# A norm aggregated early, Fourier steps placed elsewhere and stores of two images in a four-layer convolution kernel

## Chip, cores and metric

One core of one Trainium2 chip. The metric is the device time of one execution in microseconds (us), lower is better; the time before is the median of three runs.

## The reference, cut to what matters

The input is 8 images of 32 channels and 64 x 64 points. A first block makes nine softmax weights per point and filters x with them. Then four layers follow, each in this form:

```python
for j in range(4):
    z = conv3x3(x, Kj)
    z = relu(batchnorm(z, gamma[j], beta[j]))          # the first norm of the layer
    x = x + 0.1 * conv3x3T(z, Kj)
    x = batchnorm(x, gamma[j], beta[j])                # the second norm
    x = real(ifft2(fft2(x) * t))                       # t from Lj, one table for each channel
```

Both norms take mean and variance over all images and points, so each is a point where the whole tensor must be known before work with its result can begin. The second norm is an affine map per channel and the Fourier filter is linear, so the kernel may filter first and apply the affine map behind it.

## The kernel before, in words

**Tiling.** The 128 partitions hold 32 channels times 4 neighbouring image rows. Two images lie side by side, which gives four pairs (`bp` 0 to 3); a pair is cut into four chunks of 512 columns, so a convolution has 16 chunks (`c` 0 to 15). X0 and Z0 hold the data, X2 and Z2 a copy shifted by two rows, made by DMA from the SP queue (`shift_two`). A chunk of a convolution is 12 matmuls of 512 columns (24 in the profile's count, line 1102), into one of eight PSUM banks.

**Order.** `layer_steps(j)` (line 127) writes out by hand the order of one layer, and every engine walks the same list and does its own share of each step. The steps of a layer: `table` (four matmul steps for t), `norm 1`, 16 `conv2` chunks with `norm 0` (a common shift) and Fourier steps of earlier pairs between them, the second norm, and then 16 `conv1` chunks of the next layer with the Fourier steps of pairs 2 and 3 between them. The Fourier steps of a pair are `turn` (VectorE transposes, `turn`, 993), `fwdW` (PE 1250; VectorE `move_rows` 1003), `slot0` (PE 1265 and 1267; VectorE `scale_slot0` 1027), `fwdH` (PE 1281; VectorE `scale_fwdH` 1038), `slot0c` (PE 1292, ScalarE `keep_slot0` 665), `invH` (PE 1309, in the last layer 1306; VectorE `move_slots` 1009), `invW` (PE 1324) and `back` (VectorE `move_back` 1020). GpSimd mixes the halves of a pair ahead of `turn` (`mix_halves`, 498) and unmixes them behind `back` (`unmix_halves`, 508). `affine` is ScalarE's scaling by the second norm (`scale_x`, 684; for pair 0 `scale_first`, 696), `copied` is VectorE's scaling of X2 for pair 0 (`scale_copy`, 959 and 961).

**Banks.** `number_banks` gives each step of the list the next bank; `fwdW` and `invW` begin at a multiple of four. Before a matmul step writes a bank, `claim` waits until the step that had that bank last has been read out. For an `invW` step that is `rows_back`, so `back` on VectorE; for `fwdW` it is `rows_moved`.

**First norm.** For each of the 16 chunks VectorE takes `bn_stats` (851, for the last chunk 847 out of PSUM), then `aggregate` (889) runs `bn_aggr` over all 96 values and one product (892), PE averages over the four row groups (1223), and `scale_and_bias` (909) makes scale and bias, with a square root by ScalarE (`root`, 624) in the middle. Then `relu_first` (942, VectorE) and `relu_pair` (641, ScalarE) produce what `conv2` chunk 0 reads.

**Second norm.** ScalarE sums squares of each chunk (`sum_x`, 659). `moments` is `aggregate_x` (894) on VectorE, `norm 2` is the average on PE and `scale_and_bias` on VectorE. On ScalarE the square root of `norm 2` is not taken at the step `norm 2`, but at the step `affine 0`:

```python
def scale_x(j, bp):
    if bp == 0:
        root(j, 2)
        act.wait_ge(bn_ready, 2 * j + 2)
```

`conv1` chunk 0 of the next layer waits for the first part of `scale_first` and for the first `copied`.

**Stores.** At the end SP stores pairs 0 to 2 and three quarters of pair 3, one DMA for one image and one of four partition groups, 36 in all; ScalarE's queue stores the last quarter with 4.

Of the kernel before, what the change touches and what calls it, by code (L numbers as in the profile page):

```python
# [32 lines left out]
WORK = 2048  # L33
SL = W // 2
# [84 lines left out]
def fourier(j, bp, what, some=range(Q)):  # L119

    steps = quarters(what, j, bp, some)
    if what == "fwdH":
        steps = [("slot0", j, bp)] + steps + [("scaled", j, bp)]
    return steps


def layer_steps(j):

    steps = [("table", j, 0), ("table", j, 1), ("norm", j, 1), ("table", j, 2), ("table", j, 3)]
    after = {  # L130
        1: [("norm", j, 0)],
        6: fourier(j, 0, "fwdW"),
        8: fourier(j, 0, "fwdH") + [("slot0c", j, 0)],
        9: fourier(j, 1, "fwdW"),
        10: fourier(j, 0, "invH"),
        11: fourier(j, 1, "fwdH") + [("slot0c", j, 1)],
        12: fourier(j, 0, "invW") + [("back", j, 0, 0), ("back", j, 0, 1)],
        13: fourier(j, 1, "invH"),
        14: fourier(j, 2, "fwdW"),
    }  # L140
# [12 lines left out]
    steps += [("scaled", j, 2, 1), ("turn", j, BP - 1, 0), ("turn", j, BP - 1, 1), ("weights", j)]  # L153
    rest = {
        0: [("slot0c", j, 2)],
        2: fourier(j, 2, "invH") + [("affine", j, 1)],
        3: fourier(j, 3, "fwdW"),
        4: fourier(j, 2, "invW") + [("back", j, 2, 0), ("back", j, 2, 1)],
        5: fourier(j, 3, "fwdH") + [("slot0c", j, 3), ("affine", j, 2)],
        6: fourier(j, 3, "invH"),  # L160
        7: fourier(j, 3, "invW") + [("back", j, 3, 0), ("back", j, 3, 1)],
        9: [("affine", j, 3)],
    }
    for c in range(NCH):
        steps += [("conv1", j + 1, c)] + rest.get(c, [])
    return steps


def last_steps(j):

    steps = fourier(j, 2, "fwdH") + [("slot0c", j, 2), ("turn", j, BP - 1, 0), ("turn", j, BP - 1, 1)] + fourier(j, 1, "invW")
    steps += [("back", j, 1, 0), ("back", j, 1, 1)] + fourier(j, 3, "fwdW") + fourier(j, 2, "invH")
    steps += fourier(j, 3, "fwdH") + [("slot0c", j, 3), ("moments", j), ("norm", j, 2), ("affine", j, 0), ("affine", j, 1)]
    steps += fourier(j, 2, "invW") + [("back", j, 2, 0), ("back", j, 2, 1)] + fourier(j, 3, "invH") + fourier(j, 3, "invW")
    return steps + [("back", j, 3, 0), ("back", j, 3, 1), ("affine", j, 2), ("affine", j, 3)]
# [38 lines left out]
def build(nc, x_in, par, w1, b1, w2, b2, cst, sel, idb, out):  # L214
# [3 lines left out]
    with ExitStack() as ctx:  # L218
# [29 lines left out]
        sums = sb("sums", 2 * NCH)  # L248
        backw = (backw0, spare[:, 0:WORK])
# [16 lines left out]

        def leaving(bp, image, l, n, p0=0, p1=128):

            o = bp * REG2 + G * W * image + W * l
            return Z2[p0:p1, o:o + W * n]  # L270

        def bank(n):
            return psum[:, n % BANKS, :]
# [40 lines left out]
        copy_scaled = sem("copy_scaled")  # L314
        rows_turned = sem("rows_turned")
# [80 lines left out]
        def store(eng, bp, image, l, n):  # L396

            for q in range(R):
                to = out[2 * bp + image].rearrange("c (q l) w -> q c (l w)", q=R)[q]
                eng.dma_start(to[:, W * l:W * l + W * n],  # L400
                              leaving(bp, image, l, n, C * q, C * q + C)).then_inc(out_done, 16)
# [13 lines left out]
        def _(sp):  # L415
# [37 lines left out]
            for bp in range(BP - 1):  # L453
                sp.wait_ge(x_back, NCH * (DEPTH - 1) + Q * bp + Q)
                for image in range(2):
                    store(sp, bp, image, 0, G)
            for h in range(2):
                sp.wait_ge(x_back, NCH * DEPTH - Q + 2 * h + 2)
                store(sp, BP - 1, 0, G // 2 * h, G // 2)
                if h == 0:  # L460
                    store(sp, BP - 1, 1, 0, G // 2)
            sp.wait_ge(out_done, 16 * (2 * R * (BP - 1) + 4 * R))

        @block.gpsimd
        def _(pool):
# [25 lines left out]
            def mix_halves(j, bp, i):  # L491

                bk.result(NUMBER["conv2", j, bp * Q + 2 + i])
                if bp == BP - 1 and i == 1 and j + 1 < DEPTH:
                    pool.wait_ge(copy_scaled, 3 * j + 2)
# [14 lines left out]
            for j in range(DEPTH):  # L510
                for what, *at in layer_steps(j):
                    if what == "conv2" and at[1] % Q > 1:
                        mix_halves(j, at[1] // Q, at[1] % Q - 2)
                    elif what == "back" and j + 1 < DEPTH and at[2] == 1:
                        unmix_halves(*at[:2])

        @block.scalar
        def _(act):
# [202 lines left out]
            store(act, BP - 1, 1, G // 2, G // 2)  # L721

        @block.vector
        def _(dve):
# [60 lines left out]
            nc.vector.memset(part, 0.0).then_inc(part_zeroed, 1)  # L785
            v = X2[:, :].rearrange("p (b s) -> p b s", s=REG2)
# [55 lines left out]

            def conv1_stats(j, c):
                n = NUMBER["conv1", j, c]
                if c == NCH - 1:
                    bk.full(n)
                    nc.vector.bn_stats(stats[:, 6 * c:6 * c + 6], bank(n)).then_inc(last_stats, 1)
                    dve.wait_ge(last_stats, j + 1)
                    return
                bk.result(n)  # L850
                nc.vector.bn_stats(stats[:, 6 * c:6 * c + 6], rows(Z0, REG, c // Q, CH * (c % Q), CH))  # L851
# [48 lines left out]
            def common_shift(j):  # L900

                n = NUMBER["norm", j, 0]
                bk.full(n)
                nc.vector.tensor_scalar(S(26), bank(n)[:, 0:1], -1.0, None, ALU.mult)
                nc.vector.tensor_scalar(S(32), bank(n)[:, 0:1], 1.0, None, ALU.mult).then_inc(drained[n % BANKS], 1)
                bk.result(n)
                dve.sem_inc(shift_ready, 1)

            def scale_and_bias(j, which):
# [12 lines left out]
                else:  # L922
                    nc.vector.tensor_scalar(small[:, 30:32], bank(n)[:, 0:2], 1.0 / (NCH * N), None, ALU.mult)\
                        .then_inc(drained[n % BANKS], 1)
                    bk.result(n)
                    step(nc.vector.tensor_scalar(S(29), S(30), S(26), None, ALU.add))
                    link(nc.vector.scalar_tensor_tensor(S(33), in0=S(30), scalar=-1.0, in1=S(32), op0=ALU.mult, op1=ALU.add))
# [23 lines left out]
            def scale_copy(j, i):  # L951
# [5 lines left out]
                if i == 0:  # L957
                    z = rows(X2, REG2, 0, 0, 1, 0, 2 * C, 128)
                    nc.vector.tensor_scalar(z, z, small[2 * C:128, 12:13], small[2 * C:128, 13:14], ALU.mult, ALU.add)
# [80 lines left out]
            for j in range(DEPTH):  # L1040
                aggregate()
                for what, *at in layer_steps(j):
# [31 lines left out]
                    elif what == "scaled":  # L1074
                        if at[1] == 0:
                            dve.wait_ge(table_done, 4 * (j + 1))
                        if len(at) == 2:
                            scale_slot0(*at)
                        for h in at[2:] or (0, 1):
                            for q in (2 * h, 2 * h + 1):  # L1080
                                scale_fwdH(j, Q * at[1] + q)
                        if at[2:] == [0]:
                            scale_slot0(j, at[1])
# [6 lines left out]
        def _(pe):  # L1090
# [16 lines left out]
            def conv1(j, c):  # L1107
                if c == 0:
                    pe.wait_ge(weights_ready, 2 * j if j else 1)
                    if j == 0:  # L1110
                        pe.wait_ge(edges_x, 2)
                if j and c < 3:
# [360 lines left out]
```

## Time and profile before

| what | value |
|---|---|
| runs | 685.67, 687.19, 690.33 us; median 687.19 us |
| the profiled execution's own time | 689.43 us |
| its span in the trace | 687.6 us |
| PE busy with matmuls | 621.9 us (90%) |
| VectorE (DVE) busy | 495.0 us (72%) |
| ScalarE (ACT) busy | 299.7 us (44%) |
| GpSimd (POOL) busy | 234.0 us (34%) |

Times in rows of a timeline are us from the span's start, then the duration, the engine, the line, the operation and the tiles. A bracket at the end tells how long the engine was idle before and what released it. "x4" is the number of instructions merged in one row; a row can overlap the next. In rows by group the columns are line, engine, operation, tiles, count, then busy us and mean ns of one, then the idle time before them with its releasers.

### The profile page before, as it was taken

What the parts mean: (1) busy time and instruction counts of PE and PEld (TensorE: products, weight loads), DVE (VectorE), ACT (ScalarE), POOL (GpSimd) and SP (SyncE); (2) the same over time, 40 slices, a digit from 0 to 9 for tenths busy, and PEclk for the clock granted to TensorE, in tenths of its full rate; (3) what the DMA queues carried; (4) which work ended last, traced back from release to release, by engine and by line L of the source; (5) the groups of instructions that cost most, each with busy time, mean ns of one, the idle gap of its engine ahead of it and who ended that gap; (6) DMA issues with size and microseconds to landing.
All of it is one profiled execution on the core that took longest, in us unless ns stands there. A gap on an engine that the chain in (4) does not pass through costs nothing.

```text
span 687.6 us, 14558 instructions
## 1 busy us (share of the span) xinstructions
PE 621.9 (90%) x5848; PEld 196.5 (29%) x5848; DVE 495.0 (72%) x940; ACT 299.7 (44%) x518; POOL 234.0 (34%) x180
## 2 busy tenths in 40 slices
PE   5597999999999989999999899999999999999881
PEld 4222333222322222223322222332222323332230
DVE  3669888875687787557977865588778655876782
ACT  1455666664592232338621423296114234941132
POOL 0367666673042441401424422022244220322200
PEclk9689999999999999999999999999999999999996
DMA  9996111114900112286002023930022239000017
GB/s 185 184 171 104 33 32 32 34 32 98 223 3 1 35 31 63 64 209 144 1 1 64 1 63 93 226 97 1 2 63 51 71 96 219 3 2 1 1 27 218
DMA packets 44786, 51.21 MB, mean 74 GB/s; under 512 B 36528, under 2 KB 36656, under 8 KB 42672
## 3 DMA queue, kind: packets, MB, share of 16 engines
q1 hardware_dynamic: 40240, 48.99, 32.8%
q10 hardware_dynamic: 4480, 1.30, 1.2%
q8 instruction: 47, 0.77, 0.5%
q14 instruction: 19, 0.16, 0.1%
HBM read 11.99 MB, written 4.19 MB: 24 GB/s over the span
## 4 chain that ended last, share of the span: by engine, by line
PE 54%; DVE 25%; ACT 5%; POOL 5%; issue 5%; DMA 3%; SPq 1%; DVEq 0%; ACTq 0%; POOLq 0%
PE psum L1102 28%; PE psum L1177 6%; DVE work L1003 5%; POOL Z L498 5%; PE psum L1324 4%; DVE work L993 3%; DVE X L979 3%; DVE tabT L973 3%; PE psum L1128 3%; PE psum L1309 2%; PE psum L1250 2%; DMA X<-X 2%; ACT Z L638 2%; PE psum L1165 2%; PE psum L1281 1%
## 5 line engine op out<-in xcount | busy, mean ns | idle before, releaser
L1102 PE MATMUL psum<-X,wts 128*32 128x512 f32 x1536 | 176.3, 603 | 10.2 <-DVE X L961 7.0
L1102 PE MATMUL psum<-Z,wts 128*32 128x512 f32 x1536 | 173.2, 595 | 3.6 <-DVE Z L949 3.6
L498 POOL TENSOR_TENSOR Z<-X 128x512 f32<-128x512 f32 x64 | 80.7, 1283 | 247.4 <-DVE X L979 220.3
L574 ACT ACTIVATE Z<-psum 128x512 f32<-128x512 f32 x64 | 38.1, 595 | 128.9 <-PE psum L1102 117.8
L508 POOL TENSOR_TENSOR X<-Z 128x1024 f32<-128x1024 f32 x24 | 58.0, 2437 | 101.5 <-DVE Z L1020 101.5
L1102 PEld LDWEIGHTS psum<-X,wts 128*32 128x32 f32 x1536 | 47.0, 110 | 125.2 <-issue 114.7
L638 ACT ACTIVATE Z<-Z,small 128x512 f32<-128x512 f32 (+4 forms) x92 | 80.3, 922 | 4.5 <-DVE small L939 4.0
L851 DVE BATCH_NORM_STATS2 stats<-Z 128x6 f32<-128x512 f32 x60 | 41.1, 691 | 56.3 <-ACT Z L574 56.2
L1102 PEld LDWEIGHTS psum<-Z,wts 128*32 128x32 f32 x1536 | 46.9, 109 | 115.2 <-issue 107.2
L659 ACT ACTIVATE work<-X,small 128x512 bf16<-128x512 f32 x64 | 45.5, 713 | 56.3 <-DVE X L979 56.3
L979 DVE SCALAR_TENSOR_TENSOR X<-psum,X 128x512 f32<-128x512 f32 x64 | 43.6, 682 | 29.2 <-PE psum L1102 28.1
L840 DVE TENSOR_TENSOR work<-Z,psum 128x512 f32<-128x512 f32 x52 | 33.5, 679 | 19.3 <-PE psum L1165 19.2
L1020 DVE STREAM_TRANSPOSE Z<-psum 128x512 f32<-128x512 f32 x64 | 40.1, 684 | 9.9 <-PE psum L1324 9.8
L1003 DVE STREAM_TRANSPOSE work<-psum 128x512 f32<-128x512 f32 x64 | 39.9, 684 | 9.7 <-PE psum L1250 9.7
L665 ACT ACTIVATE work<-psum 128x64 f32<-128x64 f32 x16 | 4.6, 288 | 89.0 <-PE psum L1292 89.0
L1038 DVE TENSOR_TENSOR work<-psum,tabT 128x496 f32<-128x496 f32 x64 | 38.8, 661 | 2.6 <-PE psum L1281 2.2
L1177 PE MATMUL psum<-work,cstS 128*32 128x512 f32 x168 | 36.2, 628 | 2.9 <-DVE spare L840 2.7
L993 DVE STREAM_TRANSPOSE work<-Z 128x512 f32<-128x512 f32 x48 | 31.4, 701 | 5.8 <-POOL Z L498 5.5
L840 DVE TENSOR_TENSOR spare<-Z,psum 128x512 f32<-128x512 f32 x48 | 30.9, 679 | 4.8 <-PE psum L1165 4.6
L486 POOL TENSOR_TENSOR tabT<-Z,work 128x512 f32<-128x512 f32 x21 | 24.8, 1189 | 26.5 <-PE psum L1177 26.5
L1250 PE MATMUL psum<-work,cstS 32*64 32x512 f32 x384 | 31.3, 600 | 1.4 <-DVE work L993 1.4
L558 ACT ACTIVATE work<-psum 128x512 f32<-128x512 f32 x53 | 30.6, 594 | 2.9 <-ACT X L564 1.2
(136 smaller groups left out, 839.5 us busy)
## 6 DMA issues: line engine op xcount, KB each, us to landing
X<-X SPq DMA_DIRECT2D x64, 260.0 KB, 3.8
Z<-Z SPq DMA_DIRECT2D x32, 520.0 KB, 9.0
Z<-x SPq DMA_DIRECT2D x36, 128.0 KB, 4.1
out<-Z SPq DMA_DIRECT2D x24, 128.0 KB, 2.4
parS<-par SPq DMA_DIRECT2D x4, 673.0 KB, 11.5
Z<-x SPq DMA_DIRECT2D x12, 120.0 KB, 5.1
Z<-x ACTq DMA_DIRECT2D x14, 64.0 KB, 4.2
Z<-x SPq DMA_DIRECT2D x14, 64.0 KB, 4.9
```

Source lines behind the costliest of these rows:

```text
L498: nc.gpsimd.tensor_tensor(rows(Z0, REG, bp, CH * (2 * half + i), CH), low, high, op=op)\
L508: nc.gpsimd.tensor_tensor(dst, even, odd, op=op).then_inc(parts_added, 1)
L638: last = nc.scalar.activation(z, z, ACT.Relu, bias=small[p0:p1, 13:14], scale=small[p0:p1, 12:13])
L659: nc.scalar.activation(by_row(rest[:, o:o + N // 2].bitcast(bf16)), xc, ACT.Square, bias=small[:, 26:27], accum_out=sums[:, NCH + c:NCH + ...
L840: nc.vector.tensor_tensor(by_line(product(c, dj, r)), around(c, dj, r), by_line(bank(n)), op=ALU.mult)\
L851: nc.vector.bn_stats(stats[:, 6 * c:6 * c + 6], rows(Z0, REG, c // Q, CH * (c % Q), CH))
L979: nc.vector.scalar_tensor_tensor(xc, in0=by_row(bank(n)), scalar=STEP, in1=xc, op0=ALU.mult, op1=ALU.add, accum_out=sums[:, c:c + 1]).then ...
L993: last = nc.vector.transpose(dst[:, b], src.rearrange("p g (e l b) -> p b g e l", e=2, b=2)[:, b])
L1003: nc.vector.transpose(freqw[:, N * q:N * q + N], src).then_inc(rows_moved, 1)
L1102: last = nc.tensor.matmul(out_b[C * r:C * r + C, :], weights[:, o:o + C], rows(src, reg, bp, g, CH, dj - 1), start=(dj == 0), stop=(dj == ...
L1177: last = nc.tensor.matmul(bank(n)[C * r:C * r + C, :], cm(C_STACK, C), product(c, dj, r), start=(dj == 0), stop=(dj == 2), tile_position=( ...
L1250: last = nc.tensor.matmul(bank(first + r)[64 * half:64 * half + 64, :], cstS[k, C_FW + 64 * hi:C_FW + 64 * hi + 64], src[:, hi], start=(hi ...
```

## The change

1. First norm: `bn_stats` of the last chunk goes to a tile of its own, `merged`. Behind chunk 14 `merge_groups` aggregates the first 15 chunks (90 values) and writes mean and spread as two groups of `HALF_COUNT` elements; `aggregate` then runs over 12 values. `norm 1` moves from behind `table 1` to behind `table 0`.
2. `slot0` is a step of its own, and its scaling by VectorE goes with it: behind `conv2` chunks 8 and 11, ahead of `turn`. `scaled` holds `scale_fwdH` alone.
3. Between the layers: `moments` and `norm 2` stand ahead of `invW` of pair 1; `slot0c` of pair 2 stands ahead of `affine 0` instead of behind `conv1` chunk 0; the Fourier steps between `conv1` chunks stand one chunk earlier, `affine 3` too; `weights` moves behind chunk 7.
4. The top edge row of X2 for pair 0 is scaled by GpSimd (`scale_edge`, a semaphore `edge_scaled` that `conv1` chunk 0 waits for) and not by VectorE; GpSimd's last `mix_halves` of a layer is issued behind it.
5. In the last layer `moments` follows `slot0c 2`, and `norm 2` and `affine 0` stand ahead of `back` of pair 1. Before, they stood behind `slot0c 3`.
6. A store takes both images: 16 DMAs on SP and 4 on ScalarE's queue, each of twice the bytes.
7. `scale_and_bias` for `norm 2` takes the shifted mean straight from the bank, and S(32) is gone.

```diff
     steps = quarters(what, j, bp, some)
     if what == "fwdH":
-        steps = [("slot0", j, bp)] + steps + [("scaled", j, bp)]
+        steps.append(("scaled", j, bp, *some))
...
-    steps = [("table", j, 0), ("table", j, 1), ("norm", j, 1), ("table", j, 2), ("table", j, 3)]
+    steps = [("table", j, 0), ("norm", j, 1), ("table", j, 1), ("table", j, 2), ("table", j, 3)]
...
         steps.append(("conv2", j, c))
+        if c in (8, 11):
+            steps.append(("slot0", j, int(c == 11)))
...
-    steps += quarters("fwdH", j, 2, (0, 1)) + [("slot0", j, 2), ("scaled", j, 2, 0)] + fourier(j, 1, "invW")
-    steps += [("moments", j), ("norm", j, 2)] + quarters("fwdH", j, 2, (2, 3))
-    steps += [("affine", j, 0), ("copied", j, 0), ("copied", j, 1), ("back", j, 1, 0), ("back", j, 1, 1), ("copied", j, 2)]
-    steps += [("scaled", j, 2, 1), ("turn", j, BP - 1, 0), ("turn", j, BP - 1, 1), ("weights", j)]
+    steps += fourier(j, 2, "fwdH", (0, 1)) + [("slot0", j, 2), ("moments", j), ("norm", j, 2)] + fourier(j, 1, "invW")
+    steps += quarters("fwdH", j, 2, (2, 3)) + [("slot0c", j, 2), ("affine", j, 0), ("copied", j, 0), ("copied", j, 1)]
+    steps += [("back", j, 1, 0), ("back", j, 1, 1), ("copied", j, 2), ("scaled", j, 2, 2, 3), ("turn", j, BP - 1, 0), ("turn", j, BP - 1, 1)]
...
-    steps = fourier(j, 2, "fwdH") + [("slot0c", j, 2), ("turn", j, BP - 1, 0), ("turn", j, BP - 1, 1)] + fourier(j, 1, "invW")
-    steps += [("back", j, 1, 0), ("back", j, 1, 1)] + fourier(j, 3, "fwdW") + fourier(j, 2, "invH")
-    steps += fourier(j, 3, "fwdH") + [("slot0c", j, 3), ("moments", j), ("norm", j, 2), ("affine", j, 0), ("affine", j, 1)]
+    steps = [("slot0", j, 2)] + fourier(j, 2, "fwdH") + [("slot0c", j, 2), ("moments", j)]
+    steps += [("turn", j, BP - 1, 0), ("turn", j, BP - 1, 1)] + fourier(j, 1, "invW") + [("norm", j, 2), ("affine", j, 0)]
+    steps += [("back", j, 1, 0), ("back", j, 1, 1), ("affine", j, 1)] + fourier(j, 3, "fwdW") + fourier(j, 2, "invH")
+    steps += [("slot0", j, 3)] + fourier(j, 3, "fwdH") + [("slot0c", j, 3)]
...
+            def scale_edge(j):
+
+                pool.wait_ge(bn_ready, 2 * j + 2)
+                pool.wait_ge(x2_in[0][0], 32 * (j + 2))
+                pool.wait_ge(halves_mixed, Q * (BP * j + BP - 1) + 2)
+                z = rows(X2, REG2, 0, 0, 1, 0, 2 * C, 128)
+                nc.gpsimd.tensor_scalar(z, z, small[2 * C:128, 12:13], small[2 * C:128, 13:14], ALU.mult, ALU.add)\
+                    .then_inc(edge_scaled, 1)
...
+            def merge_groups():
+
+                twice = merged[:, 0:6].rearrange("p (g k) -> p k g", k=3)
+                link(nc.vector.bn_aggr(small[:, 36:38], stats[:, 0:6 * (NCH - 1)]))
+                nc.vector.tensor_scalar(twice[:, 1], small[:, 36:37].broadcast_to([128, 2]), 1.0, None, ALU.mult)
+                step(nc.vector.tensor_scalar(twice[:, 2], small[:, 37:38].broadcast_to([128, 2]), HALF_COUNT, None, ALU.mult))
...
-                link(nc.vector.bn_aggr(small[:, 0:2], stats[:, :]))
+                dve.wait_ge(link_s, count[0])
+                link(nc.vector.bn_aggr(small[:, 0:2], merged[:, :]))
```

## Rows read from the trace of the kernel before

**Rows 1.** Stretch, length, busy us of PE, PEld, DVE, ACT, POOL, clock, DMA share, GB/s.

```profile
182.00:293.00 111.00, 106.09 (x1088) 32.05 (x1092) 85.33 (x161) 48.08 (x81) 39.07 (x24) 1.00 0.18 45
```

**Rows 2.** Groups by line and shape, of PE, VectorE and GpSimd, over the span.

```profile
L1102 PE MATMUL psum<-X,wts 128*32 128x512 f32 x1536 | 176.3, 603 | 10.2 <-DVE X L961 7.0 <-DMA X<-X 3.2
...
L1292 PE MATMUL psum<-work,cstS 64*64 64x32 f32 x128 | 6.5, 218 | 7.4 <-DVE work L1027 7.4
...
L917 DVE BATCH_NORM_AGGREGATE small<-small 128x2 f32<-128x6 f32 x4 | 0.7, 182 | 0.0
...
L498 POOL TENSOR_TENSOR Z<-X 128x512 f32<-128x512 f32 x64 | 80.7, 1283 | 247.4 <-DVE X L979 220.3 <-DVE X L961 27.1
```

**Rows 3.** Timeline at the first norm of the third layer.

```profile
442.20 0.59 DVE L891 BATCH_NORM_AGGREGATE small<-stats 128x2 f32<-128x96 f32 x1
...
442.83 0.23 DVE L892 TENSOR_SCALAR small<-cstS,small 128x4 f32<-128x4 f32 x1
...
443.76 0.39 PE L1223 MATMUL psum<-small,cstS 128*128 128x5 f32 x2
...
447.38 4.93 PE L1102 MATMUL psum<-Z,wts 128*32 128x512 f32 x44 [0.90 <-DVE Z L949]
```

**Rows 4.** Timeline behind conv2 chunk 11 of the third layer.

```profile
490.77 1.31 DVE L993 STREAM_TRANSPOSE work<-Z 128x512 f32<-128x512 f32 x2 [1.39 <-POOL Z L498]
492.00 0.18 DVE L1027 TENSOR_TENSOR work<-psum,tabT 128x64 f32<-128x64 f32 x1
492.11 2.40 DVE L1038 TENSOR_TENSOR work<-psum,tabT 128x496 f32<-128x496 f32 x4
492.33 0.42 PE L1292 MATMUL psum<-work,cstS 64*64 64x32 f32 x8 [1.30 <-DVE work L1027]
...
492.79 0.28 ACT L665 ACTIVATE work<-psum 128x64 f32<-128x64 f32 x1 [11.76 <-PE psum L1292]
...
495.40 1.95 PE L1324 MATMUL psum<-work,cstS 64*32 64x512 f32 x32
```

**Rows 5.** Timeline between the second layer's conv2 and the third's conv1.

```profile
377.43 1.95 PE L1324 MATMUL psum<-spare,cstS 64*32 64x512 f32 x32
...
378.24 0.18 DVE L897 TENSOR_REDUCE small<-sums 128x2 f32<-128x32 f32 x1
379.31 0.38 PE L1223 MATMUL psum<-small,cstS 128*128 128x2 f32 x2
379.62 1.06 PE L1281 MATMUL psum<-work,cstS 64*64 64x496 f32 x8
...
380.56 0.29 ACT L624 ACTIVATE small<-small 128x1 f32<-128x1 f32 x1 [3.26 <-DVE small L928]
...
381.86 0.35 DVE L959 TENSOR_SCALAR X<-X,small 64x128 f32<-64x128 f32 x1
382.22 1.00 DVE L961 TENSOR_SCALAR X<-X,small 128x512 f32<-128x512 f32 x2
383.03 4.47 PE L1102 MATMUL psum<-X,wts 128*32 128x512 f32 x24 [2.34 <-DVE X L961]
```

**Rows 6.** PE alone in stretches: length, busy us (count), granted clock, DMA share, GB/s.

```profile
252.00:253.00 1.00, 1.00 (x16) 1.00 0.02 8
...
517.00:518.00 1.00, 1.00 (x8) 0.50 0.00 0
```

**Rows 7.** Timeline at conv1 chunk 12 of the third layer.

```profile
430.89 10.52 PE L1102 MATMUL psum<-X,wts 128*32 128x512 f32 x96 [0.99 <-DMA X<-X]
```

**Rows 8.** Timeline of the last layer's end.

```profile
652.70 2.47 DVE L1020 STREAM_TRANSPOSE Z<-psum 128x512 f32<-128x512 f32 x4
...
663.22 3.47 PE L1324 MATMUL psum<-work,cstS 64*32 64x512 f32 x32 [0.18 <-issue]
...
667.65 18.28 SPq L400 DMA_DIRECT2D out<-Z  x36
...
675.42 2.44 ACT L684 ACTIVATE Z<-Z,small 128x1024 f32<-128x1024 f32 x2 [3.27 <-DVE Z L1020]
```

More of the change, by code:

```diff
@@ L33 @@
 WORK = 2048
+HALF_COUNT = (NCH - 1) * CH * ROW / 2
 SL = W // 2
@@ L149, in layer_steps @@
         return steps + last_steps(j)
-    steps += quarters("fwdH", j, 2, (0, 1)) + [("slot0", j, 2), ("scaled", j, 2, 0)] + fourier(j, 1, "invW")
-    steps += [("moments", j), ("norm", j, 2)] + quarters("fwdH", j, 2, (2, 3))
-    steps += [("affine", j, 0), ("copied", j, 0), ("copied", j, 1), ("back", j, 1, 0), ("back", j, 1, 1), ("copied", j, 2)]
-    steps += [("scaled", j, 2, 1), ("turn", j, BP - 1, 0), ("turn", j, BP - 1, 1), ("weights", j)]
+    steps += fourier(j, 2, "fwdH", (0, 1)) + [("slot0", j, 2), ("moments", j), ("norm", j, 2)] + fourier(j, 1, "invW")
+    steps += quarters("fwdH", j, 2, (2, 3)) + [("slot0c", j, 2), ("affine", j, 0), ("copied", j, 0), ("copied", j, 1)]
+    steps += [("back", j, 1, 0), ("back", j, 1, 1), ("copied", j, 2), ("scaled", j, 2, 2, 3), ("turn", j, BP - 1, 0), ("turn", j, BP - 1, 1)]
     rest = {
[L155 to L162, printed above, removed]
+        1: fourier(j, 2, "invH") + [("affine", j, 1)],
+        2: fourier(j, 3, "fwdW"),
+        3: fourier(j, 2, "invW") + [("back", j, 2, 0), ("back", j, 2, 1)],
+        4: [("slot0", j, 3)] + fourier(j, 3, "fwdH") + [("slot0c", j, 3), ("affine", j, 2)],
+        5: fourier(j, 3, "invH"),
+        6: fourier(j, 3, "invW") + [("back", j, 3, 0), ("back", j, 3, 1)],
+        7: [("weights", j)],
+        8: [("affine", j, 3)],
     }
@@ L454, in _ @@
                 sp.wait_ge(x_back, NCH * (DEPTH - 1) + Q * bp + Q)
[L455 to L462, printed above, removed]
+                store(sp, bp, 0, G)
+            sp.wait_ge(x_back, NCH * DEPTH - Q + 2)
+            store(sp, BP - 1, 0, G // 2)
+            sp.wait_ge(out_done, 16 * R * (BP + 1))
         @block.gpsimd
@@ L511, in _ @@
                 for what, *at in layer_steps(j):
-                    if what == "conv2" and at[1] % Q > 1:
+                    if what == "copied" and at[1] == 0:
+                        scale_edge(j)
+                    elif what == "copied" and at[1] == 1:
+                        pool.wait_ge(copy_scaled, 3 * j + 2)
+                        pool.wait_ge(edge_scaled, j + 1)
+                        mix_halves(j, BP - 1, 1)
+                    elif what == "conv2" and at[1] % Q > 1 and (at[1] < NCH - 1 or j == DEPTH - 1):
                         mix_halves(j, at[1] // Q, at[1] % Q - 2)
@@ L850, in conv1_stats @@
                 bk.result(n)
-                nc.vector.bn_stats(stats[:, 6 * c:6 * c + 6], rows(Z0, REG, c // Q, CH * (c % Q), CH))
+                last = nc.vector.bn_stats(stats[:, 6 * c:6 * c + 6], rows(Z0, REG, c // Q, CH * (c % Q), CH))
+                if c == NCH - 2:
+                    link(last)
+                    merge_groups()
             for i in range(2):
@@ L1073, in _ @@
                         scale_copy(*at)
-                    elif what == "scaled":
+                    elif what == "slot0":
                         if at[1] == 0:
                             dve.wait_ge(table_done, 4 * (j + 1))
[L1077 to L1083, printed above, removed]
+                        scale_slot0(*at)
+                    elif what == "scaled":
+                        for q in at[2:]:
+                            scale_fwdH(j, Q * at[1] + q)
                     elif what == "conv1":
```

35 lines of the change are left out of this document (16 added, 19 removed).

## The prediction

> **What bounds the kernel now.** I read the stages first, then who waits in them, then the timeline at each wait. In the first layer's stretch behind the first norm PE works 106.09 of 111 us and VectorE 85.33 [rows 1]: PE sets the pace, and only its pauses can be won. The groups with idle time before them name the pauses that the change can touch [rows 2]: conv1 matmuls wait 7.0 us for the second norm and 3.2 us for a DMA, both over three layer boundaries, and `slot0c` waits 7.4 us for `scale_slot0`, over four layers of two places. A fourth pause, 0.90 us behind the first norm, occurs once a layer [rows 3]. The end is not set by compute: ScalarE's last scaling ends at 677.86, but SP issues 36 stores from 667.65 to 685.93, 0.51 us each, and the span ends at 687.6 [rows 8].
>
> **First norm (items 1).** `bn_aggr` over 96 values takes 0.59 us [rows 3]; over 6 values it takes 0.18 [rows 2], so over 12 about 0.21 by the slope between them. The product of line 892 then starts 0.38 us earlier and ends at 442.68 instead of 443.06. Before, that gained nothing, since the average stood behind `table 1` and ran at 443.76; now it stands one table step earlier (a table is some 1.2 us of PE, so `table 0` ends at about 442.55) and runs at about 442.8: 0.96 earlier. Scale, bias and the first relu follow by as much. But PE was busy until 447.38 - 0.90 = 446.48 with tables and average, and that work stays; it gets a pause of about 0.25 ahead of the average. So `conv2` starts at about 446.75, not 447.38: 0.63 us a layer, four layers: -2.5 us. Bounds: 0 and -3.6 (the whole pause). The aggregate of 15 chunks and two small operations (about 0.56 us, and at most 0.23 each by line 892) stand ahead of the last chunk's `bn_stats` on VectorE, which waits for PE anyway; without that cover they would cost 1.0 us a layer.
>
> **slot0 a step earlier (item 2).** In [rows 4] `scale_slot0` runs at 492.00 because it stands behind `turn`, which waited for GpSimd; PE pauses 1.30 us for it. Placed ahead of `turn` it falls into VectorE's own pause of 1.39 us there and costs nothing. What is late next: `invW` of pair 0 claims banks that `scale_fwdH` must empty. That ends at 492.11 + 2.40, less the 0.11 that `slot0` took, so 494.4, and `invW` starts at about 494.5 instead of 495.40: 0.9 of the 1.30 is won. At the other place nothing is late next and the pause, 7.4 / 4 - 1.30 = 0.55 us, is won whole. Sum -1.45 a layer, -5.8 us; bounds 0 (next wait takes it all) and -7.4.
>
> **Between the layers (items 3, 4, 7).** This is where I expect the change to work against itself. `norm 2` on PE now waits for `moments`, which ends at 378.42; with 0.15 us from VectorE to PE (492.18 to 492.33 in [rows 4]) it runs at 378.57, not 379.31, and PE pauses 1.1 us from 377.43. Behind it come `invW` (about 1.9), the two `fwdH` steps (1.0) and now `slot0c`, which thus starts at about 378.57 + 0.33 + 1.88 + 0.99 = 381.77 [rows 5]. ScalarE walks the same list: `keep_slot0` of pair 2 now stands ahead of `affine 0`, and the square root of the norm is taken in `affine 0`. So the root waits for `slot0c`. By [rows 4] `keep_slot0` starts 0.46 us behind `slot0c` and takes 0.28; ScalarE's operations overlap, so the root runs between 382.25 and 382.5, I take 382.3, not 380.56, 1.74 us later although its input is there at about 379.7. VectorE waits for it inside `scale_and_bias`, and with it everything to `conv1` chunk 0. VectorE no longer scales the edge row (0.35 us), but then ScalarE's first part is the last to come, so that I credit 0.1. `conv1` chunk 0 starts at 383.03 + 1.64. `slot0c` is no longer behind it: -0.35. The wait for the DMA at `conv1` chunk 12 (0.99 to 1.02) [rows 7] goes, because `affine 3` and its transfer come one chunk (10.52 / 4 = 2.6 us) earlier and the transfer's lateness was 1.0: -1.0. Net +1.64 - 0.35 - 1.0 = +0.3, over three boundaries +0.9 us. Bounds a boundary: -2.2 if the root did not wait (the norm 0.75 earlier, plus 0.1 + 0.35 + 1.0) and +1.4 if the DMA wait stayed and the edge row came 0.1 late. `weights` (1.47 us of VectorE) moves to where VectorE waits for `conv1` chunks: 0.
>
> The edge row on GpSimd: 512 columns with two inputs take 1.28 us [rows 2], so 128 columns with one input lie between 0.32 and 1.28; I take 0.4, nearest in work per column. It starts 0.15 behind the norm and ends before ScalarE's first 0.81 us: nothing. VectorE's two copies run in the same 1.0 us [rows 5]. The Trainium skill (SBUF — State Buffer, "SBUF: two separate sides") says that a VectorE operation in a two-port mode and a GpSimd operation exclude each other for a whole instruction. By that the edge row would come behind both copies, at 1.4 us, and chunk 0 0.5 us later: +1.5 in all; no row here shows this pair, and the sum goes without it.
>
> **Clock.** At this place the clock is half in two of three boundaries: behind equal pauses the row at 252 us shows 1.00, the one at 517 us 0.50 [rows 6], and chunk 0 takes 4.47 us, not 2.7 [rows 5]. The pause ahead of chunk 0 stays (2.6 instead of 2.34), so I expect no change: 0, bounds -3.4 (never, 2 x 1.7) and +1.7 (all three).
>
> **The end (items 5, 6).** Before, `back 1` runs 652.70 to 655.17 [rows 8] and `fwdW` of pair 3 beside it. Now the average moves one bank on and `fwdW` gets the four banks of `invW 1`, so it must wait for `back 1`; and VectorE stands in `scale_and_bias` (379.69 to 381.8, so 2.1 us [rows 5]) between the last `turn` and `back 1`. `back 1` ends at about 657.5, `fwdW` then starts on an engine that paused 5.7 us, at half clock 3.6 us instead of 1.9 as `invW` did at 663.22 (3.47) [rows 8], so `move_rows` starts at 661.3, not straight behind `back 1` at 655.1: 6.2 late. Given back are 2.8 us: the norm's 2.1 no longer stand between `scale_fwdH` of pair 3 and `back 2`, and `invW 2` runs at full clock. ScalarE's last scaling ends 3.4 us later, at 681.3. But then only ScalarE's four stores are left (4 x 0.51; SP's part is issued in 16 x 0.51 us and long gone), and with 2.1 to 2.8 us from the last issue to the end the span ends at about 685.3: -2.3 us. Bounds: -5.7 (no bank wait, end at 677.86 + 4) and +1.
>
> **Sum.** -2.5 - 5.8 + 0.9 - 2.3 = -9.7 us. The profiled execution took 689.43, so it would take 679.7; it is 2.24 above the median, so the median goes from 687.19 to 677.5 (-1.4%).
>
> **The rivals.**
> (a) *The root is not held up, or a free boundary wins.* If `slot0c` came before the root's input, the boundary gave -2.2 instead of +0.3, and with shorter pauses the clock would hold (-3.4): 677.5 - 7.5 - 3.4 = 667 us. For it: all inputs of the norm are 0.75 us earlier. Against it: the order of ScalarE's steps, which is fixed by the list.
> (b) *The slot0 pauses are only moved.* VectorE has the same work, and PE would meet it at the next step: item 2 gives 0, and 683.3 us. For it: `invW` would have to wait at once. Against it: VectorE is busy only 85 of 111 us there.
> (c) *The clock falls at both pauses of a boundary* (the other side). If it fell at the new pause of 1.1 us ahead of `norm 2`, the 3.2 us of work up to `slot0c` would run at half rate, 3.2 us on the path at each of three boundaries, and the boundary without half clock so far would pay 1.7: +11.3, 689 us, slower than before. It decides from 9.7 / 3 = 3.2 us a boundary on. Against it: pauses of 1.30 us inside `conv2` are followed by matmuls of normal length (1.95 us for `invW`) [rows 4].
>
> **How the numbers follow.** Forecast 0.70, (a) 0.10, (b) 0.14, (c) 0.06. The forecast's own range is 673.5 to 681.5, from the clock (-3.4, +1.7), the end and the edge row. The range for 8 in 10 reaches to (b) and leaves (a) and (c) out: 672 to 684. One per cent, about what a measurement tells from no change, is 6.9 us, so faster means below 680.3: nine tenths of the forecast and (a), 0.72; within 1%: the rest of the forecast, (b) and most of (c), 0.24; slower 0.04.
>
> **What would show it.** First norm: line 1223 about 1 us earlier against the last `conv1` matmul, pause ahead of `conv2` below 0.3. slot0: no wait of 1292 for 1027; a new one of about 0.3 of `invW` for 1038. Boundary: the root (624) right behind `keep_slot0` (665), and a pause of about 2.5 us ahead of `conv1` chunk 0; no wait for the X DMA. End: line 1250 waits for 1020 for over 5 us, and the last stores are ScalarE's. I am wrong if the root precedes `keep_slot0`, or if the waits ahead of conv1 shrink.

## The result and the profile after

The changed kernel takes 683.21 us (median of 12 runs, 679.38 to 686.70) beside 687.83 us for the kernel before in the same comparison: ratio 0.994, interval 0.9924 to 0.9955, so 4.1 us (0.6%) faster. The forecast was 677.5 us, in a range of 672 to 684: the direction was right, the gain less than half of it. The profiled execution took 683.50 us with a span of 681.7, against 689.43 and 687.6 before: 5.9 us less, where the sum had said 9.7. So of the 5.7 us between 677.5 and 683.21 the traces hold 3.8. The rest is no work of the kernel: the execution traced before lies 1.6 us above the median of its twelve runs and the one traced now 0.3 above its own (1.3 us), and that median is 687.83 us and not the 687.19 of three runs (0.6 us).

Groups over the span of the changed kernel first, by line and shape (line 1117 is the former 1102).

```profile
L1117 PE MATMUL psum<-X,wts 128*32 128x512 f32 x1536 | 176.7, 608 | 7.5 <-ACT X L705 7.4
L1117 PE MATMUL psum<-Z,wts 128*32 128x512 f32 x1536 | 173.2, 595 | 0.0
```

The wait for the X DMA is gone, the wait ahead of `conv2` too, and `slot0c` waits for nothing any more. But the wait ahead of conv1 chunk 0 is still there (7.4 us for 7.0 in [rows 2]), and it is now for ScalarE. The second boundary between layers, as a timeline (1240 is the average, 1341 `invW`, 1298 `fwdH`, 674 `keep_slot0`, 633 the root, 705 and 979 the scaling, 501 the edge row):

```profile
375.64 0.35 PE L1240 MATMUL psum<-small,cstS 128*128 128x2 f32 x2 [1.07 <-DVE small L918]
376.09 3.40 PE L1341 MATMUL psum<-spare,cstS 64*32 64x512 f32 x32
379.42 1.25 PE L1298 MATMUL psum<-work,cstS 64*64 64x496 f32 x8
...
380.92 0.28 ACT L674 ACTIVATE work<-psum 128x64 f32<-128x64 f32 x1 [6.55 <-PE psum L1309]
381.04 0.29 ACT L633 ACTIVATE small<-small 128x1 f32<-128x1 f32 x1
...
382.33 3.04 ACT L705 ACTIVATE X<-X,small 128x512 f32<-128x512 f32 x4 [1.00 <-DVE small L960]
382.33 1.07 DVE L979 TENSOR_SCALAR X<-X,small 128x512 f32<-128x512 f32 x2
382.40 0.72 POOL L501 TENSOR_SCALAR X<-X,small 64x128 f32<-64x128 f32 x1 [10.89 <-DVE small L960]
...
383.35 6.13 PE L1117 MATMUL psum<-X,wts 128*32 128x512 f32 x40 [2.48 <-ACT X L705]
```

Against [rows 5]: PE pauses for 1.07 us ahead of the average (forecast 1.1), the root stands directly behind `keep_slot0` (forecast so), and the pause ahead of chunk 0 is 2.48 us (forecast 2.6). What is not as in the forecast is the duration of `invW`: 3.40 us, not 1.9. PE alone, in stretches of 1 us of the same place (length, busy, then the granted clock as a share of 2.4 GHz):

```profile
376.00:377.00 1.00, 0.91 (x16) 0.72 0.00 0
377.00:378.00 1.00, 1.00 (x16) 0.50 0.06 16
378.00:379.00 1.00, 1.00 (x16) 0.50 0.00 0
379.00:380.00 1.00, 1.00 (x12) 0.57 0.00 0
380.00:381.00 1.00, 0.87 (x16) 1.00 0.00 0
383.00:384.00 1.00, 0.65 (x4) 0.64 0.02 8
384.00:385.00 1.00, 1.00 (x8) 0.50 0.00 0
```

The clock falls to 1.2 GHz twice at one boundary: behind the pause at the average and behind the pause ahead of chunk 0. The third boundary shows the same; the first only the second fall.

The end (1038 is `back`, 1267 `fwdW`, 1021 `move_rows`, 693 the last scaling, 401 the stores):

```profile
650.81 2.50 DVE L1038 STREAM_TRANSPOSE Z<-psum 128x512 f32<-128x512 f32 x4
...
653.38 24.53 SPq L401 DMA_DIRECT2D out<-Z  x16
653.57 3.31 PE L1267 MATMUL psum<-work,cstS 32*64 32x512 f32 x32 [5.78 <-DVE Z L1038]
...
657.20 2.51 DVE L1021 STREAM_TRANSPOSE work<-psum 128x512 f32<-128x512 f32 x4 [3.88 <-PE psum L1267]
...
674.91 2.44 ACT L693 ACTIVATE Z<-Z,small 128x1024 f32<-128x1024 f32 x2 [4.71 <-DVE Z L1038]
677.38 1.88 ACTq L401 DMA_DIRECT2D out<-Z  x4
```

**Where the 5.9 us are.** The two averages per layer on PE are marks that both traces have. The next table takes the start of the average of `norm 0` (the former line 1223 with one column) in each layer, so a period holds a boundary, a conv1, a first norm and the beginning of a conv2.

| stretch | before | after | difference | forecast |
|---|---|---|---|---|
| start to norm 0 of layer 1 | 187.33 | 186.63 | -0.70 | -0.63 |
| to layer 2 | 131.81 | 131.01 | -0.80 | -1.78 |
| to layer 3 | 133.53 | 132.84 | -0.69 | -1.78 |
| to layer 4 | 133.33 | 132.89 | -0.44 | -1.78 |
| norm 0 of layer 4 to the end | 101.60 | 98.33 | -3.27 | -3.75 |
| sum | 687.6 | 681.7 | -5.9 | -9.7 |

The beginning and the end are within 0.5 us, the beginning by luck in part: it holds the first block, which no edit touches and which differs by up to 6 us between traces. The three periods between hold the error: 3.4 us.

### The profile page after: what moved, and what is told of

Read it like the earlier page. It is cut to its first block, busy times and chain, and to the rows that moved or that the text cites. A ratio compares the mean times of both kernels' runs of the same rounds, so it can differ in the third digit from the quotient of the medians.

```text
span 681.7 us, 14557 instructions
## 1 busy us (share of the span) xinstructions
PE 624.1 (92%) x5848; PEld 199.0 (29%) x5848; DVE 501.6 (74%) x946; ACT 299.9 (44%) x518; POOL 236.2 (35%) x183
## 3 DMA queue, kind: packets, MB, share of 16 engines
HBM read 11.99 MB, written 4.19 MB: 24 GB/s over the span
## 4 chain that ended last, share of the span: by engine, by line
PE 81%; DVE 11%; issue 3%; ACT 2%; DMA 1%; SPq 1%; POOL 0%; DVEq 0%; ACTq 0%; POOLq 0%
PE psum L1117 47%; PE psum L1194 6%; PE psum L1267 5%; PE psum L1341 5%; PE psum L1298 4%; PE psum L1326 3%; DVE work L1021 3%; PE psum L1145 3%; PE psum L1182 2%; DVE work L1056 1%; PE psum L1323 1%; PE psum L1225 1%; PE psum L1227 1%; DVE work L850 1%; PE psum L1159 1%
## 5 line engine op out<-in xcount | busy, mean ns | idle before, releaser
L1267 PE MATMUL psum<-work,cstS 32*64 32x512 f32 x384 | 32.7, 631 | 5.8 <-DVE Z L1038 5.8
L1298 PE MATMUL psum<-work,cstS 64*64 64x496 f32 x256 | 31.7, 602 | 0.5 <-DVE work L1021 0.5
```

Of the source, the lines that this page charges most:

```text
L1267: last = nc.tensor.matmul(bank(first + r)[64 * half:64 * half + 64, :], cstS[k, C_FW + 64 * hi:C_FW + 64 * hi + 64], src[:, hi], start=(hi ...
L1298: last = nc.tensor.matmul(bank(first + x)[half:half + 64, 0:16 * (SL - 1)], cstS[k, C_FH:C_FH + 64], src, start=True, stop=True, tile_posi ...
```

## The experiments

Each kernel was timed beside the kernel before; a ratio is to that kernel, with its 95% interval in brackets. The theory: the error is the clock, which falls at the new pause at the average (rival (c), in two boundaries of three), and beside it the root in ScalarE's queue costs what the forecast said. The rival theory: the conv stages or other waits lost the time.

**Filling the pause at the average.**

```diff
                 bk.claim(n)
+                if which == 2 and j + 1 < DEPTH:
+                    nc.tensor.matmul(bank(n), cm(C_AVG), cstS[:, 0:N], start=True, stop=True)
```

> The changed kernel with one dummy matmul of 512 columns on constants, into the bank that norm 2 has claimed, ahead of the wait for `moments` at the three layer boundaries. It fills most of the pause of 1.07 us. Theory (the loss against the forecast is the clock, halved from the average of norm 2 to slot0c at the second and third layer boundary, 376 to 380 and 509 to 513 us): granted clock 1.00 in these stretches, invW 1.9 us instead of 3.4, 1.6 us saved twice, 3.2 us faster than the changed kernel, ratio to the kernel before 0.989 to 0.990. Rival (the clock there costs nothing, since the root waits for something else, or the loss is in the conv stages): same as the changed kernel within 0.5 us, 0.994.

677.24 us, ratio 0.9855 (0.9831 to 0.9880), against 0.994 without the dummy. One matmul more at each boundary (two in the profile's count), and the kernel is some 6 us faster. Its second boundary as a timeline, and then PE's stretches with the granted clock:

```profile
372.67 1.13 PE L1236 MATMUL psum<-cstS 128*128 128x512 f32 x2
373.72 0.38 PE L1242 MATMUL psum<-small,cstS 128*128 128x2 f32 x2
374.15 1.95 PE L1343 MATMUL psum<-spare,cstS 64*32 64x512 f32 x32
```

```profile
374.00:375.00 1.00, 0.96 (x17) 1.00 0.00 0
375.00:376.00 1.00, 1.00 (x24) 1.00 0.00 0
376.00:377.00 1.00, 1.00 (x20) 1.00 0.00 0
```

`invW` takes 1.95 us again. The gain is larger than the 3.2 forecast. In this trace the periods are 131.14, 130.97 and 129.69 us, 4.9 less in sum than the changed kernel's: the first, where the clock had not fallen at the average, is as in the changed kernel, and the third is shorter by more than the fall at the average, because it kept the full clock in chunk 0 as well. Whether the dummy did that is not shown; the run with norm 2 of the last layer ahead of the turns (below) has no dummy and kept the full clock in its first chunk 0 too.

**Filling the pause ahead of chunk 0 too.**

```diff
                 if j and c == 0:
+                    bk.claim(NUMBER["conv1", j, 0])
+                    for i in range(2):
+                        nc.tensor.matmul(bank(NUMBER["conv1", j, 0]), cm(C_AVG), cstS[:, 0:N], start=True, stop=True)
```

> As the run before, and two dummy matmuls of 512 columns more ahead of conv1 chunk 0 of layers 2 to 4, in the pause of 2.48 us. Theory: the clock stays at 1.00 in conv1 chunk 0 too, 4.4 us become 2.7, 1.7 us saved at each of three boundaries on top of the 3.2: 8.3 us faster than the changed kernel, ratio about 0.982. Rival (a pause before the matmuls is not what halves the clock): chunk 0 still takes 4.4 us, ratio as the run before.

674.58 us, ratio 0.9814 (0.9791 to 0.9837). The granted clock stayed at 1.00 from layer 1's first norm to the pause ahead of `fwdW` of pair 3 in the last layer; the periods are 129.69, 129.70 and 129.82 us. So in the changed kernel's trace the clock costs 1.3, 3.1 and 3.1 us in the three periods, 7.5 in all: 1.3 for a fall ahead of chunk 0 alone, and 1.8 more where it fell at the average as well.

**The kernel before with the same dummies ahead of chunk 0.**

> The kernel before with two dummy matmuls of 512 columns on constants ahead of conv1 chunk 0 of layers 2 to 4, in its pause of 2.34 us. It prices the half clock in the kernel before. By its profile (two of three boundaries at half clock, 1.5 and 1.7 us): 3.3 us faster, ratio 0.995, clock 1.00 at all three boundaries. Other view (the half clock there is not on the path): 1.000.

683.35 us, ratio 0.9939 (0.9918 to 0.9960). Periods 131.62, 131.76 and 131.64: the trace before is longer by 0.2, 1.8 and 1.7, 3.7 us. The 1.8 and 1.7 are its two half clocks; in the first period the clock had not fallen, and 0.2 is how far such a difference can be off. With this the account closes. With the clock up on both sides the change is worth 131.67 - 129.74 = 1.93 us a period, and the forecast had said 1.78. The clock took back 7.5 - 3.7 = 3.8 us of the three periods' 5.8. The timed runs say the same without any trace: with the dummies on both sides the change is worth 0.9814 / 0.9939, some 8.7 us give or take 2, beside the 9.7 of the forecast and the 4.1 without dummies.

**The root ahead of keep_slot0.**

```diff
                 if bp == 0:
-                    root(j, 2)
                     act.wait_ge(bn_ready, 2 * j + 2)
...
+                    elif (what, at) == ("norm", [j, 2]):
+                        root(j, 2)
                     elif what == "slot0c":
```

> The changed kernel, but ScalarE takes the square root of the second norm at the step norm 2 and not at affine 0, so ahead of keep_slot0 of pair 2. Theory (the root waits in ScalarE's queue behind keep_slot0, which waits for slot0c on PE): the root runs about 4 us earlier (at 377 instead of 381 in the second boundary), the pause of 2.48 us ahead of conv1 chunk 0 shrinks below 0.3 at all three boundaries, and the half clock in chunk 0 goes: 3 x 2.3 + 3 x 1.7 = 12 us faster than the changed kernel, 671 us, ratio 0.976. Rival 1 (VectorE or the transfers hold conv1 chunk 0 anyway): the pause stays above 1.5 us and the ratio above 0.990. Rival 2 (the clock, once low at the average, stays low into chunk 0): 7 us faster, ratio 0.983.

672.54 us, ratio 0.9782 (0.9761 to 0.9803). The root ran 1.3 us behind the average instead of 5.4, and the half clock in chunk 0 was gone. But the pause did not fall below 0.3:

```profile
376.20 0.28 ACT L674 ACTIVATE work<-psum 128x64 f32<-128x64 f32 x1 [3.70 <-PE psum L1310]
376.32 3.03 ACT L704 ACTIVATE X<-X,small 128x512 f32<-128x512 f32 x4
377.33 1.93 PE L1118 MATMUL psum<-X,wts 128*32 128x512 f32 x16 [1.18 <-issue]
```

Scale and bias were there at 373.5 in this run, but `keep_slot0` (674) still stood in ScalarE's queue ahead of the scaling (704). I had moved one of the two instructions that mattered. In all three boundaries the clock stayed up behind this pause of 1.18 us.

**Two neighbouring steps exchanged.**

```diff
-    ... + [("slot0c", j, 2), ("affine", j, 0), ("copied", j, 0), ...
+    ... + [("affine", j, 0), ("slot0c", j, 2), ("copied", j, 0), ...
```

> The changed kernel with two neighbouring steps of the list exchanged between the layers: affine 0 ahead of slot0c 2. PE's order stays as it is; ScalarE takes the root and scales X0 of pair 0 ahead of keep_slot0, which in the run with the early root alone still held the scaling until 376.32 us. Theory (ScalarE's place of keep_slot0 is all that holds conv1 chunk 0): the pause ahead of chunk 0 falls from 2.48 us in the changed kernel and 1.18 us in that run to below 0.3, the half clock behind the average of norm 2 stays in two of three boundaries; 3 x 1.1 = 3.3 us faster than that run, about 669 us, ratio 0.973 to 0.975. Rival (the edge row on GpSimd or the copies on VectorE come next): a pause of 1 us stays, ratio 0.978.

668.71 us, ratio 0.9726 (0.9702 to 0.9750), 14.5 us less than the changed kernel, by an exchange that leaves PE's order as it is. In the traces the three periods are 12.1 us shorter (128.54, 128.84 and 127.26):

```profile
369.04 0.35 PE L1240 MATMUL psum<-small,cstS 128*128 128x2 f32 x2 [1.07 <-DVE small L918]
369.49 2.90 PE L1341 MATMUL psum<-spare,cstS 64*32 64x512 f32 x32
...
370.33 0.29 ACT L633 ACTIVATE small<-small 128x1 f32<-128x1 f32 x1 [2.55 <-DVE small L949]
...
371.63 3.04 ACT L705 ACTIVATE X<-X,small 128x512 f32<-128x512 f32 x4 [1.00 <-DVE small L960]
...
373.90 0.37 PE L1309 MATMUL psum<-work,cstS 64*64 64x32 f32 x8
374.20 4.07 PE L1117 MATMUL psum<-X,wts 128*32 128x512 f32 x36
```

PE goes from `slot0c` (1309) to chunk 0 (1117) with no pause. The half clock behind the average is still there (`invW` 2.90), in two of three boundaries. So the early second norm was worth having; ScalarE's queue kept it from being used.

**The end in the old order.** The last layer's steps as before (`moments`, `norm 2` behind `slot0c 3`), all else as changed.

> The changed kernel with the last layer's end in the order of the kernel before (moments and norm 2 behind slot0c 3, so that fwdW of pair 3 doesn't get the banks of invW 1), stores of two images kept. Theory (the early norm costs compute 3.5 us in the end: 5.8 us pause of fwdW for back 1 and half clock, less what is given back): ScalarE's last scaling ends 3.5 us earlier and the span 3.4 us earlier than in the changed kernel, ratio 0.989. Rival (all stores now fall into the last 14 us and their bandwidth sets the end): less than 1 us faster, or slower; the DMA queue is busy to the end.

682.75 us, ratio 0.9925 (0.9906 to 0.9944): no difference from the changed kernel's 0.994 that the intervals would separate. The theory was right on compute and the rival on the end. ScalarE's last scaling starts 28.6 us behind the last `fwdH` of pair 2 (641.92), not 32.05 as in the changed kernel, so 3.45 us earlier as forecast:

```profile
662.78 15.15 SPq L400 DMA_DIRECT2D out<-Z  x16
...
670.52 2.44 ACT L692 ACTIVATE Z<-Z,small 128x1024 f32<-128x1024 f32 x2 [3.24 <-DVE Z L1037]
672.99 4.13 ACTq L400 DMA_DIRECT2D out<-Z  x4
```

Yet ScalarE's four stores take 4.13 us to issue, not 1.88, and the span ends 8.1 us behind their start, not 4.3: from norm 0 to the end it is 98.62 us, beside 98.33. All 4.19 MB leave in 16.7 us (the first packet starts at 663.6, the last ends at 680.3), some 250 GB/s, with the DMA engines busy nine tenths. The early norm costs compute and lets the stores begin 10 us earlier; the two cancel.

**Norm 2 of the last layer ahead of the turns**, so that `fwdW` of pair 3 gets other banks than `invW 1`:

```diff
-    steps = [..., ("slot0c", j, 2), ("moments", j)]
-    steps += [("turn", ...), ("turn", ...)] + fourier(j, 1, "invW") + [("norm", j, 2), ("affine", j, 0)]
+    steps = [..., ("slot0c", j, 2), ("moments", j), ("norm", j, 2)]
+    steps += [("turn", ...), ("turn", ...)] + fourier(j, 1, "invW") + [("affine", j, 0)]
```

> The changed kernel, in the last layer with norm 2 ahead of the turns of pair 3 and invW of pair 1: fwdW of pair 3 then gets banks that invW 1 doesn't use. Theory (the claim on back 1 costs): the wait of fwdW 3 for back 1 (5.8 us) becomes one for turn 3 of about 3 us, ScalarE's last scaling comes 1.8 us earlier against the start of the last fwdH of pair 2, the stores still begin early; 1.8 us faster than the changed kernel, ratio 0.991. Rival (the norm's chain on VectorE costs the same wherever it stands): no difference, 0.994.

680.46 us, ratio 0.9894 (0.9868 to 0.9921). `fwdW` no longer waits for `back 1`:

```profile
653.05 2.53 PE L1267 MATMUL psum<-work,cstS 32*64 32x512 f32 x32 [2.62 <-DVE work L1011]
...
674.55 2.44 ACT L693 ACTIVATE Z<-Z,small 128x1024 f32<-128x1024 f32 x2 [4.71 <-DVE Z L1038]
```

From the last `fwdH` of pair 2 (644.29) to the scaling it is 30.26 us, against 32.05: 1.8 as forecast, and norm 0 to the end is 96.55 us against 98.33. The ratio, 3.2 us below the changed kernel's, shows more than that, but the intervals of the two allow 1.8 as well.

**Item 2 alone, and with the clock held up.** The split of `slot0` for pairs 0 and 1 in the kernel before (its scaling on VectorE moves with it, not printed here):

```diff
-        steps = [("slot0", j, bp)] + steps + [("scaled", j, bp)]
+        steps = ([("slot0", j, bp)] if bp > 1 else []) + steps + [("scaled", j, bp)]
...
         steps.append(("conv2", j, c))
+        if c in (8, 11):
+            steps.append(("slot0", j, int(c == 11)))
```

> The kernel before with item 2 alone for pairs 0 and 1 (slot0 and its scaling behind conv2 chunks 8 and 11, ahead of the turns). Forecast: 0.55 + 0.9 us a layer, 5.8 us faster, ratio 0.9916. By the pauses that the changed kernel's trace leaves (0.66 us ahead of invW of pair 0): 0.55 + 0.65 a layer, 4.8 us, 0.993. Rival (the pauses are only moved): 1.000.

> The same dummy matmuls with item 2 in the kernel before. The run of item 2 alone gave 7.8 us where its pauses explain 4.8; its profile had one boundary at half clock. Theory (the rest is the clock, which falls or not at a pause of 2.3 us by chance of its place in time): with the clock held up in both kernels item 2 is worth 4.8 us, so 0.988 if the run before gives 0.995. Rival (item 2 saves 7.8 us in itself): 0.984.

680.07 us, ratio 0.9886 (0.9857 to 0.9915), which is more than either of the two numbers expected, and with the dummies 677.59 us, 0.9845 (0.9820 to 0.9870). Against the dummies alone (0.9939) item 2 is worth 0.0094, 6.5 us, between my 4.8 and 7.8; the times don't separate the two. The traces tell it more exactly. From the average of norm 0 to that of norm 2 a layer takes 60.17 to 60.23 us in the kernel before and 58.75 to 58.79 in both runs with item 2, in the first three layers: 1.40 us, four times 5.6. The forecast was 1.45. What item 2 alone gained beyond 5.6 us lies outside this stretch, as far as its trace shows: it has one boundary at half clock, the kernel before two, and it reached the first average 2.4 us sooner, in a part that the edit does not touch.

**Item 1 alone** (`merge_groups`, `merged`, average behind `table 0`).

> The kernel before with item 1 alone (15 chunks aggregated ahead, average behind table 0). Forecast and what the changed kernel's pauses show (0.90 us ahead of conv2 gone, 0.21 to 0.34 ahead of the average): 0.65 us a layer, 2.6 us, ratio 0.996. Rival (hidden behind the tables): 1.000.

684.72 us, ratio 0.9952 (0.9933 to 0.9970). Its three periods are 132.77, 132.87 and 132.81, all with the half clock; the two such periods of the kernel before are 133.53 and 133.33: 0.61 us a layer, forecast 0.63.

**Item 6 alone**, stores of two images in the kernel before.

> The kernel before with item 6 alone, stores of two images. Theory A (SP's issue of 36 stores at 0.51 us each sets the end): the end is ScalarE's last scaling plus 4.3 us, 682.2 instead of 687.6, 5.4 us faster, ratio 0.992. Theory B (16 DMA engines need 16.5 us for 4.19 MB from the first store on, as in the run with the old order of the end): 2.3 us faster, ratio 0.9966. Against both: no difference.

686.77 us, ratio 0.9980 (0.9965 to 0.9995): about 1.4 us. From the last norm 2 to the end it is 23.0 us instead of 24.9. The gain is near that of theory B (2.3), far from A's 5.4.

```profile
665.40 14.87 SPq L401 DMA_DIRECT2D out<-Z  x16
...
673.07 2.44 ACT L680 ACTIVATE Z<-Z,small 128x1024 f32<-128x1024 f32 x2 [3.17 <-DVE Z L1016]
675.54 3.75 ACTq L401 DMA_DIRECT2D out<-Z  x4
```

16 issues take 14.87 us, where 36 took 18.28. Of the 16, twelve are of 256 KB and four of 128 KB; of the 36, the first 24 were of 128 KB and the last 12 of 64 KB. Two groups of eight stores in the trace of the kernel before, first of 128 KB, then of 64 KB, each with a stretch near it whose last two numbers are the DMA engines' share and GB/s (columns as in [rows 1]):

```profile
670.59 3.73 SPq L400 DMA_DIRECT2D out<-Z  x8
671.00:674.00 3.00, 1.95 (x32) 0.58 (x32) 0.77 (x2) 1.16 (x2) 0.00 (x0) 1.00 0.90 272
682.22 3.72 SPq L400 DMA_DIRECT2D out<-Z  x8
683.00:686.00 3.00, 0.00 (x0) 0.00 (x0) 0.00 (x0) 0.00 (x0) 0.00 (x0) 0.50 0.53 137
```

Both go at 0.47 us a store. So in the kernel before the issue does set the pace of the last, small stores, and the DMA engines are half idle beside them (0.53); with 128 KB they are nine tenths busy at the same pace. With the larger stores SP's issue takes 0.95 us in the median of the 16, the DMA engines are busy 0.85 to 0.96 of the time from 669 to 681 us, and the packets need 16.5 us instead of 18.4: then the transfers seem to set the pace. That is why fewer issues gained 1.9 us here and not 5.4.

**Put together**: the exchange, norm 2 ahead of the turns in the last layer, and the dummy at the average.

> Put together: the changed kernel with affine 0 ahead of slot0c 2, norm 2 of the last layer ahead of the turns, and one dummy matmul in the pause ahead of norm 2 between the layers. The first gave 668.7 us, the second 1.8 us in compute, the dummy should hold the clock where two of three boundaries lose 1.6 us (3.2): 663.5 us, ratio 0.965. Rival (with the pauses shorter the clock costs nothing more there): 667 us, 0.970.

664.17 us, ratio 0.9648 (0.9628 to 0.9669), 3.5% faster than the kernel before, where the change alone had brought 0.6%. Its periods are 127.33, 127.24 and 127.57 us. In its second boundary:

```profile
366.82 1.13 PE L1236 MATMUL psum<-cstS 128*128 128x512 f32 x2
367.86 0.38 PE L1242 MATMUL psum<-small,cstS 128*128 128x2 f32 x2
368.44 1.95 PE L1343 MATMUL psum<-spare,cstS 64*32 64x512 f32 x32 [0.20 <-issue]
370.32 1.06 PE L1300 MATMUL psum<-work,cstS 64*64 64x496 f32 x8
371.20 0.37 PE L1311 MATMUL psum<-work,cstS 64*64 64x32 f32 x8
371.50 4.93 PE L1117 MATMUL psum<-X,wts 128*32 128x512 f32 x44
```

## Why the prediction was wrong, step by step

**First norm: right.** PE's pause ahead of the average is 0.21 us, in the first layer 0.33 (forecast 0.25), that ahead of `conv2` is gone, and item 1 alone gives 0.61 us a layer (0.63).

**slot0: right in the sum, partly by luck.** 1.40 us a layer (1.45). The new wait of `invW` of pair 0 that I named is there, 0.66 us instead of 0.4, and at the other place 0.08 us stays: the pauses give only 1.1 us a layer. The other 0.3 lie in PE's busy time between the two averages (58.2 us before, 57.9 with item 2), which I had not counted. Rival (b), pauses only moved, is out, although its number, 683.3 us, is the one that was measured; that is chance.

**Between the layers: the waits right, the net a little too dear.** The root behind `keep_slot0`, the pauses of 1.07 and 2.48 us and the lost DMA wait came as forecast. With the clock up, a period (first norm, `slot0` and boundary together) came to -1.93, forecast -1.78. The run with two steps exchanged shows that the queue on ScalarE was the cause of the pause: it is the one thing of the order that it changes.

**Clock: the step that failed.** I wrote "I expect no change: 0", and gave rival (c), a fall at the pause of 1.1 us, a chance of 0.06, because pauses of 1.30 us inside `conv2` are followed by matmuls of normal length [rows 4]. The fall came in two of three boundaries. By the periods with the clock held up, the clock took 1.1 us more in the first period (the fall ahead of chunk 0 was new there), and 1.4 in the second and in the third (the new fall at the average, 1.8, less 0.4, by which the one ahead of chunk 0 was cheaper than before): 3.9 us, of which 0.45 came back since the waits were a little better than forecast. That is the 3.4 that the three periods lack. The traced execution is no oddity: the mean granted clock was 0.962 to 0.969 in the twelve runs of the changed kernel and 0.967 to 0.972 in the runs of the kernel before beside the experiments. To compare pauses by their length alone was the error. The one of 1.30 us inside `conv2` lies between `fwdH` and the eight matmuls of `slot0c` with a conv chunk behind them; this one has the six matmuls of `slot0` ahead of it and only the average behind it before `invW` begins. Whether that difference is why was not tried by itself; that the pause is the cause was: with one dummy matmul in it the clock fell there in none of the nine boundaries of three traces, without it in ten of fifteen of five traces. My bound for the clock, +1.7 for a half clock ahead of chunk 0 in all three boundaries, left out the case that the rival described. The rival's own price was too high: 3.2 us for a fall at the average, where it cost 1.8, since the clock was back before `slot0c` (the row at 380 us shows 1.00).

**The end: right in size (-1.9 after item 2's share, forecast -2.3), partly for a wrong reason.** The claim on `invW 1`'s banks, the 5.78 us pause and the half clock came as forecast, and the last scaling came 3.4 us late to within 0.1. But the sum took the end before for a matter of issues alone, 0.51 us each, to be had back by making fewer. The two runs with all stores of two images at the end (item 6 alone, and the old order of the end) show that 4.19 MB in one go take 16.5 and 16.7 us with 20 stores, where 40 took 18.4; cutting them otherwise is worth 1.9 us. What the change gained beyond that is that half of them leave early.

**The edge row.** Scaling it took 0.72 us on GpSimd (forecast 0.4) and ended at 383.12, before the second of VectorE's copies (383.40), which took 1.07 us together instead of 1.00. So it did not come behind both copies, and the +1.5 us did not come. By the Trainium skill (SBUF — State Buffer, "SBUF: two separate sides") the exclusion lasts for one instruction; to put the edge row behind both copies was my reading, and goes beyond it. The second copy took 0.61 us here, 0.54 in the kernel before. The trace cannot tell whether the edge row ran between the copies, as exclusion for one instruction would have it, or beside them. Either way it ended ahead of ScalarE's first part.

What stays open: why the clock falls at a pause in one boundary and not in the next of the same run. At the average the clock fell in the second and third boundary of the changed kernel, and in the first and second of the kernel with the two steps exchanged; the pause of 2.34 us left the clock up in one of the three boundaries of the kernel before, in two of three with item 2 alone, in none with item 1 or item 6 alone. And the first block, which no edit touches, ends up to 6 us apart between traces (first average at 173.4 to 180.1 us), so single traces are good for periods, not for totals.

## What to carry to other kernels

A wait that is moved ahead of work turns that work into something late for whoever stands behind it in another engine's queue: follow the moved step on every engine's list, as here the root and the scaling behind `keep_slot0`. To exchange two steps gave 14.5 us. A pause of PE has to be priced with the clock too, its length alone did not tell here whether the clock falls, and a dummy matmul in it is a cheap way to find out. And compare stretches between marks that both traces share; totals of single executions differ here by more than most of the edits.

## What the runs showed of the hardware that was not expected

- TensorE's granted clock fell to 1.2 GHz behind a pause of 1.07 us, with `slot0` ahead of it and the average behind it, in two of three boundaries of the changed kernel and of each of the four other runs with this pause and no dummy, while the pause of 1.18 us behind `slot0c` in the run with the early root left it up three times of three; one dummy matmul of 512 columns (1.13 us) in it kept it at 2.4 GHz, and three in a boundary kept it there through both pauses.
- In the final stretch SP issued stores of 64 and of 128 KB alike every 0.47 us, at 137 and 272 GB/s; with stores of two images in one go (twelve of 256 KB, four of 128 KB) the issue took 0.95 us in the median, at some 250 GB/s.
- GpSimd took 0.72 us, beside VectorE's copies, to scale 64 x 128 elements that VectorE did in 0.35 [rows 5], 1.8 times my estimate from its 512-column rate.
